# The first ALiBi group of a two-layer transformer block takes its queries in two halves

## What is computed

```python
q, k, v = split(clip(x @ w_qkv.T, -8, 8))            # q and k are layer-normalised
scores = q @ k.T / sqrt(16) + slope[h] * (pos_k - pos_q)
scores = where(causal, scores, -inf)                  # 1024 x 1024 per head, 32 heads
probs = exp(scores - max(scores)) / sum(...)
out = (probs @ v) @ w_out.T
```

## Time and profile before

| what | us |
|---|---|
| median of 3 runs | 1565.8 (1564.93 to 1566.54) |
| the profiled execution | 1564.45 |
| its span in the trace | 1562.7 |
| PE busy | 1463.4 (94%) |
| DVE busy | 899.0 (58%) |
| ACT busy | 806.4 (52%) |
| POOL busy | 535.0 (34%) |

### The profile page before, as it was taken

One profiled execution on the slowest core, in us unless ns is written; L12 is line 12 of the kernel. 1 busy time (PEld: TensorE's weight loads), 2 busy tenths in 40 slices (PEclk: granted clock), 3 DMA queues, 4 the chain that ended last, 5 costly groups with the idle time before them and its releaser, 6 DMA issues. The chain is left out here.

```text
span 1562.7 us, 23907 instructions
## 1 busy us (share of the span) xinstructions
PE 1463.4 (94%) x8288; PEld 1025.0 (66%) x8288; DVE 899.0 (58%) x1351; ACT 806.4 (52%) x1728; POOL 535.0 (34%) x496
## 2 busy tenths in 40 slices
PE   5799999999999999999858978999999989999996
PEld 3566776776677677667636855555555548888885
DVE  4445554455555445555556637666666517777877
ACT  3555665565566565556524421555555665433433
POOL 0234444433444433344034134222232004444442
PEclk8799999999999999999979987999999999999999
DMA  5245445435544543543530034233333205000000
GB/s 189 61 47 42 40 47 51 35 46 46 43 38 48 51 34 46 44 35 38 82 61 1 1 54 68 43 59 52 56 55 56 89 13 217 1 1 0 1 28 27
DMA packets 45409, 76.16 MB, mean 49 GB/s; under 512 B 17696, under 2 KB 23328, under 8 KB 44448
## 3 DMA queue, kind: packets, MB, share of 16 engines
q1 hardware_dynamic: 40992, 64.80, 29.2%
q0 software_dynamic: 4352, 10.49, 4.4%
HBM read 42.49 MB, written 2.10 MB: 29 GB/s over the span
## 5 line engine op out<-in xcount | busy, mean ns | idle before, releaser
L682 DVE TENSOR_REDUCE nmax<-sc 128x1 f32<-128x128 f32 (+7 forms) x256 | 192.4, 752 | 150.5 <-PE sc L469 150.5
L1541 DVE TENSOR_REDUCE pm<-l_sm 128x2 f32<-128x1024 f32 (+1 forms) x192 | 179.9, 957 | 113.4 <-PE l_sm L1421 61.9
L1501 ACT ACTIVATE l_probs<-l_banks 128x512 f32<-128x512 f32 (+3 forms) x384 | 171.5, 493 | 138.1 <-PE l_banks L1445 98.8
L612 ACT COPY pt<-tb 128x512 f32<-128x512 f32 (+3 forms) x256 | 129.2, 505 | 198.3 <-PE tb L483 195.2
L604 ACT ACTIVATE probs<-sc,nmax 128x128 f32<-128x128 f32 (+7 forms) x256 | 190.6, 745 | 54.5 <-DVE nmax L682 54.3
L483 PE MATMUL tb<-ident,probs 128*128 128x128 f32 x1152 | 173.9, 276 | 2.8 <-DVE pt L690 1.1
L78 PE MATMUL sc<-k_h,q_h 128*128 128x512 f32 (+4 forms) x384 | 144.8, 377 | 14.8 <-DVE q_l L706 8.8
L1442 PE MATMUL l_banks<-qk_bufs 128*128 128x512 f32 (+3 forms) x384 | 142.4, 415 | 6.3 <-ACT l_probs L1501 3.8
L1418 PE MATMUL l_sm<-qk_bufs 128*128 128x512 f32 (+3 forms) x384 | 130.8, 412 | 12.8 <-DVE pm L1541 6.5
L507 PE MATMUL mb<-pt,ckv 128*64 128x512 f32 (+3 forms) x768 | 137.7, 494 | 0.1
L78 PE MATMUL sc<-k_l,q_h 128*128 128x512 f32 (+4 forms) x384 | 132.0, 344 | 0.0
(11 more groups left out here) (266 smaller groups left out, 3118.9 us busy)
## 6 DMA issues: line engine op xcount, KB each, us to landing
gated_late<-in_gated SPq DMA_DIRECT2D x11, 768.0 KB, 14.4
wout<-in_w_out SPq DMA_DIRECT2D x16, 512.0 KB, 7.2
late<-late SPq DMA_DIRECT2D x128, 64.0 KB, 2.0
rb<-rT SPq DMA_DIRECT2D x64, 128.0 KB, 8.8
qk_bufs<-late SPq DMA_DIRECT2D x96, 64.0 KB, 5.2
qk_bufs<-late POOLq DMA_DIRECT2D x96, 64.0 KB, 5.8
nope_t<-in_nope_by_dim SPq DMA_DIRECT2D x16, 192.0 KB, 5.6
late<-in_gated SPq DMA_DIRECT2D x3, 768.0 KB, 9.1
```

The costliest lines, as they stand in the source:

```text
L612: act.copy(pt[i // 4][:, e, j0:j0 + nb, (i % 4) * P:(i % 4 + 1) * P], tb[TB[g]][:, 0:nb, :]).then_inc(pt_act, 1)
L682: dve.tensor_reduce(nmax[:, n % 4:n % 4 + 1], row, axes, ALU.max, negate=True).then_inc(negmax, 1)
L1501: act.activation(probs[(NC * g + c) % RING][:, h, 0:w], banks[:, (E_STEPS * g + n) % SLOTS, 0:w], ACT.Exp).then_inc(exped, 1)
L1541: dve.tensor_reduce(pm[g % 2][:, :, s, i, half], slot(("m", g, n))[:, :, 0:w], AX.X, ALU.max, negate=True).then_inc(freed, 1)
```

## The change

Three things change in `alibi_order`. Six `v` tiles instead of four run before the first `m`, and the other two are cut into their four contraction steps, one after each of the first eight `m`. Group 0 visits its query rows in the order 3, 2, 1, 0, 7, 6, 5, 4 (`M_FIRST`): the first eight units (`M_HALF`) are then all of the queries 0 to 511. After those come a `top` and a `rows` of their own (`part` 0), with five more `m` around them; then chunks 0 to 3 of `e` with the eleven `m` that are left between them and `pv` 0 to 2; then the second `top` and `rows` (`part` 1) as before, and chunks 4 to 11 with all ahead items.

So that a half of the queries is one buffer row, the two query rows of a buffer hold half and head pair instead of head pair and token: `queries`, the host's `alibi_q`, and the transfers of `move` (their destination in two pieces of 512) follow. The order in `nmax` follows too. SP sends group 0's maxima in two sets of four transfers of half the size, the first set before it waits for `vp` and sends the queries of group 1; they count on a new semaphore, `rows_first`. POOL waits for the copied-out `v` (`v_ev`) and writes the value tile of group 0 first, and that of group 1 after the keys of group 1. Groups 1 to 7 keep one `top`, one `rows` and four transfers each.

```diff
+M_FIRST = [(s, i, half) for i in (3, 2, 1, 0, 7, 6, 5, 4) for half in range(i // 4 + 1) for s in range(HG // 2)]
+M_HALF = 4 * (HG // 2)
+C_HALF = 4
...
-    order = [("build", 0, 0), ("build", 0, 1)] + [("v", 0, j) for j in range(4)]
-    for n in range(NM):
-        order.append(("m", 0, n))
-        if n % 2 == 1 and n // 2 < 4:
-            order.append(("v", 0, 4 + n // 2))
-    order += [("top", 0, 0), ("m", 1, 0), ("rows", 0, 0)]
+    order = [("build", 0, 0), ("build", 0, 1)] + [("v", k, j) for j in range(6) for k in range(DK)]
+    late_v = [("v", k, j) for j in (6, 7) for k in range(DK)]
+    for n in range(M_HALF):
+        order += [("m", 0, n), late_v[n]]
+    order += [("top", 0, 0), ("m", 0, M_HALF), ("rows", 0, 0)]
+    order += [("m", 0, n) for n in range(M_HALF + 1, M_HALF + 5)]
+    rest = list(range(M_HALF + 5, NM))
+    at = 0
+    for c in range(C_HALF):
+        for h in range(HG):
+            order.append(("e", 0, HG * c + h))
+            while at < len(rest) and at * C_HALF * HG <= (HG * c + h) * len(rest):
+                order.append(("m", 0, rest[at]))
+                at += 1
+        if c >= 1:
+            order.append(("pv", 0, c - 1))
+    order += [("m", 0, n) for n in rest[at:]]
+    order += [("top", 0, 1), ("m", 1, 0), ("rows", 0, 1)]
     order += [("m", 1, n) for n in range(1, AHEAD)]
...
-        for c in range(NC):
+        for c in range(first, NC):              # first = C_HALF if g == 0 else 0
...
         def queries(b, s):
-            return keep.bufs[:, 6 * b + s, :]
+            pair = keep.bufs[:, 6 * b:6 * b + 2, :].rearrange("p a b -> p (a b)")
+            return pair.rearrange("p (half s c) -> p s half c", half=2, s=2)[:, s]
...
+                    first, count = (0, 2) if g else (part, 1)
...
-                            sp.dma_start(keep.bufs[r:r + 1, b:b + 2, :].bitcast(F32),
-                                         mT[src:src + 2 * ST, :].bitcast(F32)).then_inc(rows_in, 16)
+                            sp.dma_start(keep.bufs[r:r + 1, b:b + count, :].bitcast(F32),
+                                         mT[src:src + ST * count, :].bitcast(F32)).then_inc(rows_in if part else rows_first, 16)
...
                 sp.wait_ge(low, 1)
                 move(sp, 0, 0, moved)
+                maxima(0, 0)
                 sp.wait_ge(vp, ST)
                 move(sp, 1, 0, moved)
-                maxima(0)
+                maxima(0, 1)
...
-                    if n == 0:
-                        pe.wait_ge(rows_in, ROWS * (g + 1))
-                        if g == 0:
-                            pe.wait_ge(v_ev, ST)
+                    if g == 0 and n == 0:
+                        pe.wait_ge(rows_first, ROWS)
+                        pe.wait_ge(v_ev, ST)
+                    if n == (0 if g else HG * C_HALF):
+                        pe.wait_ge(rows_in, ROWS * (g + 1))
...
-                pool.wait_ge(vp, ST)
+                pool.wait_ge(v_ev, ST)
+                values(0, 0)
+                pool.wait_ge(vx_ok, 1)
                 for b in range(1, BUFS):
                     pads(b)
                     load_rows(b)
                     if b == 1:
                         move_keys(1)
-                pool.wait_ge(v_ev, ST)
-                for u in range(2):
-                    values(u, u)
+                        values(1, 1)
+                        pool.wait_ge(vx_ok, 2)
```

More of the change, by code:

```diff
@@ L1266, in alibi_order @@
             ahead[5:5] = [("build", g // 2 + 1, 1)]
-        done, total = 0, sum(chunk_cols(c)[1] * HG for c in range(NC))
+        first = C_HALF if g == 0 else 0
+        done, total = 0, sum(chunk_cols(c)[1] * HG for c in range(first, NC))
         at = 0
-        for c in range(NC):
+        for c in range(first, NC):
             for h in range(HG):
@@ L1347, in move @@
                     r0 = KR * (h % 2) + EX + HD1 * n
-                    eng.dma_start(dst[r0:r0 + HD1, :].bitcast(F32), stages[w][src, :]).then_inc(landed[b], 16)
+                    eng.dma_start(dst[r0:r0 + HD1].bitcast(F32),
+                                  stages[w][src, :] if which else stages[w][src, :].rearrange("p (half c) -> p half c", half=2)).then_inc(landed[b], 16)
         with nc.Block() as block:
@@ L1379, in _ @@
                     if g + 1 < GROUPS:
-                        maxima(g + 1)
+                        maxima(g + 1, 1)
             @block.tensor
@@ L1395, in build, with project_v @@
                     last.then_inc(turned, 1)
[L1397 to L1403, removed]
+                def project_v(j, k):
+                    if k == 0:
+                        from_one(pe, v_ev, j - SLOTS + 1)
+                    rows = slice(j * P, (j + 1) * P)
+                    last = three(pe, banks[:, j % SLOTS, :], [(keep.xT_h[:, k, rows], keep.wv_h[:, k, :]),
+                                                              (keep.xT_l[:, k, rows], keep.wv_h[:, k, :]),
+                                                              (keep.xT_h[:, k, rows], keep.wv_l[:, k, :])],
+                                 start=k == 0, stop=k == DK - 1)
+                    if k == DK - 1:
+                        last.then_inc(vp, 1)
                 def m(g, n):
-                    s, i, half = M_UNITS[n]
-                    c0, w = m_cols(n)
+                    s, i, half = m_unit(g, n)
+                    c0, w = m_cols(g, n)
                     b, diagonal = g % BUFS, c0 + w == (i + 1) * P
@@ L1417, in m @@
                     for par in range(2):
-                        last = pe.matmul(dst[:, par, 0:w], queries(b, s)[:, i * P:(i + 1) * P], keys(b, 2 * s + par)[:, c0:c0 + w],
+                        last = pe.matmul(dst[:, par, 0:w], query_cols(b, s, i * P, P), keys(b, 2 * s + par)[:, c0:c0 + w],
                                          start=True, stop=not diagonal)
@@ L1476, in _ @@
                     elif kind == "rows":
-                        rows(g)
+                        rows(g, n)
                     elif kind == "e":
@@ L1512, in _ @@
                         build(g, n)
-                    elif kind == "v":
+                    elif kind == "v" and g == DK - 1:
                         v_out(n)
@@ L1537, in m @@
                 def m(g, n):
[L1538 to L1539 removed]
+                    s, i, half = m_unit(g, n)
+                    w = m_cols(g, n)[1]
                     dve.wait_ge(scores, NM * g + n + 1)
```

83 lines of the change are left out of this document (48 added, 35 removed).

## The result

The changed kernel takes 1559.5 us (four runs, 1558.6 to 1560.9) against 1566.1 for the kernel before: a ratio of 0.9950, interval 0.9938 to 0.9962. It is faster by some 6 to 10 us, and the measured time lies 1.7 us above the forecast of 1557.8 and inside the range of 1553.0 to 1564.8.

What follows compares the result with a forecast made beforehand. PE bounds the main loop; the lead-in loses time to waits, low clock and the chain of maxima. Group 1 at 1007.0 instead of 1015.0 saves 8.0 us: 1556.5 profiled, forecast 1557.8, range 1553.0 to 1564.8.

Steps and rivals of the forecast that it cites:

- Parts 1 and 2: Lead-in: two more value tiles fill PE's 5.91 us wait, first `m` 930.3; eight `m` follow, last reduction about 940.2.
- Part 3: First chain of maxima in group 0: 7.8 us as before, first `e` at 948.0, 25.5 us earlier; 1.2 GHz from about 945.
- Part 4: Chunks 0 to 3 beside eleven `m`: 14.0 us plus 2.1 for the low clock, ending at 964.1.
- Part 5: Second chain of maxima in group 0: again 7.8 us, chunk 4 at 971.7; the clock falls again, 2.1 us.
- the paragraph on the queues: Moved transfer issues: group 1's moves, wanted at 964, land by 964.1 at worst, so they hide, barely.
- Part 6: Chunks 4 to 11 of group 0: 32.7 us plus 2.1 clock and 0.5 DVE; group 1 at 1007.0 instead of 1015.0.
- signs of being wrong: Low clock stretch beyond 7 us, row transfers landing late, or `m` 0 of group 1 or 2 waiting for a DMA.
- (a): Rival: the clock holds in both sparse stretches around the chains; 4.2 us less, 1553.6; chance 0.13.
- (b): Rival: the first low clock stretch lasts 20.5 us, leaving 1.35 of the 8.0 us gain, 1564.5; chance 0.17.
- (c): Rival: the second low clock stretch, over chunks 4 to 11, is as long too; slower, 1571.1; chance 0.09.
- (d): Rival: first four row transfers land late beside POOL's group 1 loads; 4.8 us later, 1562.6; chance 0.09.

Runs made afterwards that it cites:

- the repetition: The changed kernel traced and timed once more without any edit, on another occasion: 1558.6 us, 0.9943 of the kernel before.
- the kernel with value tiles and layout: The changed kernel without the split of group 0, keeping six value tiles first, the query-row layout and POOL's new order: 1561.9 us, 0.9962 of before.
- Holding the loads: The changed kernel with POOL holding its four loads for group 2 until group 1's transfers have landed: 1558.4 us, 0.9938 of before.
- moving the row issues: The changed kernel with group 0's first four row transfers issued by ACT instead of SP: 1556.7 us, 0.9934 of before.
- the kernel with the two edits together: The changed kernel with first row transfers issued by ACT and the second `rows` ahead of group 1's first `m`: 1555.2 us, 0.9926 of before.
- the kernel with the value tiles alone: The kernel before with six value tiles first and two in steps, no split, old layout: 1559.9 us, 0.9951 of before.

## Why the prediction was right

In the prediction's times, the changed kernel's being moved by the 3.7 us of its later stage:

| step | predicted | measured |
|---|---|---|
| 1: first `m` | 930.3 | 930.5 |
| 2: last reduction of the first half | 940.2 | 940.3 |
| 3: first `e` | 948.0 | 946.8 |
| 4: last reduction of group 0 | 963.9 | 960.2 |
| 5: chunk 4 | 971.7 | 971.5 |
| 6: group 1 | 1007.0 | 1006.7 |

**Parts 1 and 2** held to 0.2 us. **Part 3** was 1.3 us too long: DVE's two small copies were faster (0.17 and 0.18 us, where the only chain before had 0.61 and 0.59) and so were SP's issues (2.85 us for four instead of 3.57). The clock fell at about 948, not 945, and in the repetition it did not fall there at all.

**Part 4** was mis-sized. Chunks 0 to 3 with eleven `m` took 13.4 us, not 15.9: the clock was already back within 1 us of the first `e`, after four `m` that had kept PE busy 1.86 of 2.00 us at 1.2 GHz, and 13.0 was the better end of the bounds.

**Part 5** is the step that failed. It took 7.8 us for the second chain and got 11.3, because the paragraph on the queues said of group 1's moves that they hide, barely. Its bound for their landing was 964.1, and `m` 0 began at 964.5 on the same scale. Even this near hit is two errors that cancel: SP's row issues and twelve move issues ended 3.6 us sooner than 946.7 + 10.8, and the last landing came 10.5 us behind the last issue instead of 6.6. `m` 0 was wanted at 960.3, because parts 3 and 4 were short. In these traces the landing goes by the end of the value tiles, the row issues and the transfers' own time, and what the stretch before it saves turns into a wait, as it did without the split in the kernel with value tiles and layout. That the sum was right is therefore luck: parts 3 and 4 were put 1.3 and 2.5 us too long and part 5 3.5 us too short. Holding the loads and moving the row issues showed both shares, with 2.1 and 4.1 us less wait.

**Part 6** held as a number, 35.3 us for both, and not in its terms. The clock stayed low for 3.6 us from chunk 4's start, near the 4.2 assumed, but that cost less than the 2.1 us given to it: the kernel with the two edits together, whose clock did not fall there, took 34.4 us from chunk 4 to group 1, against 35.0 between the same exponentials here. So the clock cost some 0.7 us, and the rest took some 1 us more than the 33.2 given to it.

What the prediction valued wrongly is the split. It never priced the value tiles by themselves: it put 6.0 us of matmuls into a wait of 5.91 and let the `m` behind them run at full clock, without saying what that brings alone. It is 7.7 us (98.8 against 106.5), and the rest brings 0.5. The chain that the change adds was to be paid by exponentials that move ahead of it, and the wait inside it took that gain.

Two of its own signs of being wrong did come: a low stretch longer than 7 us (965 to 979), and `m` 0 of group 1 waiting for a DMA. Both belong to part 5.

Of the rivals, (a) came half true. In the changed kernel's first trace the clock fell in both stretches, in the repetition only in the second. It would not have been worth its 4.2 us: with the clock kept by extra matmuls, group 1 came 1.5 us earlier. By the rule on idle gaps in the Trainium skill's page "TensorE: Matmul & The Clock Gate", section "HAM oscillation — how this bites in real kernels", the clock should hold where no gap is long. The repetition agrees; the first trace does not, nor does the kernel before: the changed kernel's longest wait before its first fall was 0.91 us. (b) and (c) did not occur: low stretches of 3.4 us, and of 3.6 behind the start of chunk 4, in place of 20.5. A long one can still happen in this stage: the kernel with the value tiles alone had one of 20.5 us. (d) named the right resource at the wrong place. The row transfers landed in time, and it was the moves behind them that came late.

Left open: what the two-piece moves cost, and why the same program's clock differs at 820 to 840 us, at the first sparse stretch and in the last group.

## What to carry to other kernels

Fill a wait with work that has to be done anyway before you restructure what stands behind it: here that was 7.7 of the 8.3 us gained. When a stretch is shortened in front of something that waits for a transfer, find when that transfer can start at the earliest and land at the latest, and take the later of the two times, because a saving beyond it is lost. A split that doubles a latency chain paid here only once nothing that waits stood inside either chain: moving `rows` ahead of an `m`, and the row transfers to an idle engine's queue, made the difference.

## What the runs showed of the hardware

The clock can fall from 2.4 to 1.2 GHz though PE never waits as long as 1 us: it did at 948.1 in the changed kernel, after PE had been busy 1.40 of 2.00 us. But this is no rule: in the repetition of the same program PE was busy 1.35 and 1.53 of 2.00 us in the same place and the clock held. Two matmuls of 512 columns per reduction, whose results nobody reads, kept it up through the first group in each of the three kernels that had them and paid for themselves (1.5 to 2.8 us of the first group). The last group shows the same spread (clock 1.00 or 0.86 over the same 15 us). That moves single spans of this kernel by 2 to 4 us, as much as most edits here, so only times between marks close to the edit, or many runs, tell them apart.
